# Adaptive-norm attention block with 16 heads on one core: q and k of a pair laid out through memory off chip in nine transfers, x kept on chip, scores 20 slots ahead

## The chip, the cores and the metric

One core of a Trainium2 chip. The metric is device time in microseconds (us): 351.57 us is the median of three runs of the kernel before (351.27 to 353.29). Engines: PE is TensorE, DVE is VectorE, ACT is ScalarE, POOL is GpSimd, SP is the queue that issues most DMAs. Each engine runs its own instructions in order; semaphores order the engines among each other.

## The reference

x is (16 batches, 256 tokens, 128), cut to what matters (f32 throughout):

```
mod = (silu(c) @ wmod)                 # per batch: sa, ca, ga, sb, cb, gb of 128 each; |ga|, |gb| >= 0.25
h   = layernorm(x) * (1 + ca) + sa
q, k, v = split(h @ W_qkv + b_qkv)     # 16 heads of 8
a   = softmax(q @ k^T over keys) / sqrt(128) @ v       # per batch and head, 256 x 256 scores
x   = x + ga * (a @ W_out + b_out)
h   = layernorm(x) * (1 + cb) + sb
x   = x + gb * (fp6(h) @ fp6(weight)^T + bias)         # fp6: blocks of 32 with a scale, rounded to e2m3
```

## The kernel before

Two batches make a **pair** (8 pairs). For a pair, `transpose_x`, `project_qk` and `save_qk` give q and k with the 128 channels on the partitions and 512 tokens in a row. The scores are products in float32r; to keep precision q and k are split into a high part (`save_qk` writes it) and a low part (`low_part`), and a head's product is taken over 96 rows: three heads, of each 8 channels in four combinations of high and low, with zeros in the rows of the other two. So q and k have to be **laid out**: `k_rep` holds groups of three (or two) heads in 96 rows, `q_pad` holds each head alone in its 32 rows of 96. SP does this with DMAs (`lay_out`): 6 of k and 16 of q for a pair, after two copies that double the parts. Rows 96 and 97 of `q_pad` take minus the row maximum of the scores (high and low part), which `place_max` brings by a DMA; the matching rows of `k_rep` are ones.

The work is a software pipeline in **steps**, one for each batch b, of 16 **slots** s. In slot s of step b PE does `scores1(b+1, s)` (scores of the next batch, whose maximum DVE takes in `maxima`), `scores2(b, s)` (the scores of this batch again, transposed and with the maximum subtracted, of which ACT takes the exponential), and, at some slots, `values` (probabilities times v), the projections of the batches b-1 and b-2, and the preparation of the pair two further on (odd steps: `transpose_x` at s=0, q at s=5, k at s=8). "Step 8" below is that of b = 8. POOL splits the maxima into high and low part (`split_max`), normalises x for a coming pair (`normalise1`, even steps; its inputs are the statistics that DVE takes in `stats1` at s=4 and `aggregate1` at s=5), modulates and quantises the second half of the block, and scales weights by the modulation of the batch (`attn_weights`, `ffn_weights`).

The way of a maximum of half a batch (8 heads): `maxima` (DVE), `split_max` (POOL), `transpose_max` (PE, into the one bank `ps_pre`), `save_maxT` (ACT), `place_max` (SP, DMA), then the first `scores2` of that half waits for it (`max_placed`). Half 0 of b+1 is transposed at s=11 of step b and needed at s=0 of step b+1; half 1 is transposed at s=2 of step b+1 and needed at s=8.

SP issues in a written order: in the step of an even b it starts with the layout of the next pair (22 DMAs), into which the two `place_max`, a store and a load of the modulation row (`load_modb`, two buffers) are put. x comes in twice for each pair (`x_early`, `x_late`). Four of the pair steps run in a loop of two rounds.

The lines: `lay_out` 313 to 326, `place_max` 398 to 402, SP's order 416 to 473, `split_max` 491, `normalise1` 499, POOL's order 539 to 574, `scores1` 865, `scores2` 878, `transpose_max` 933, PE's order 981 to 1043.

## Time and profile before

| | |
|---|---|
| median of three runs | 351.57 us |
| the profiled execution, first to last instruction | 349.2 us |
| PE busy | 304.0 us (87%) |
| DVE busy | 239.4 us (69%) |
| ACT busy | 218.5 us (63%) |
| POOL busy | 173.1 us (50%) |
| granted TensorE clock, mean | 0.908 |
| first exponential, last exponential ends | 45.4 us, 332.7 us |

The profiled execution is 2.4 us below the median. A matmul's end is modelled, so that busy PE means that matmuls are in flight, not that PE is at its peak. The granted clock is 1.00 at 2.4 GHz and 0.50 at 1.2 GHz. Windows below have the instructions of each engine in brackets behind its busy time.

### The profile page before, as it was taken

The page shows a single profiled execution, that of the slowest core. Times are in us where ns is not written, and L with a number is a line of the kernel's source. Part 1 is how long each engine was busy: PE and PEld are TensorE (multiplying, and loading weights), DVE is VectorE, ACT ScalarE, POOL GpSimd, SP SyncE. Part 2 cuts the span into 40 slices and gives each one's busy share as a digit, 9 for nine tenths or more (in the row PEclk, how much of TensorE's full clock was granted, in tenths as well). Part 3 has the DMA queues.
Part 4 walks back from the last instruction along what each step waited for, and adds up shares of the span by engine and source line. Part 5 has one row for each costly group of instructions (what it writes and reads, how often), then busy time and mean ns, then how long its engine had stood idle before and what let it go on. Part 6 is the DMA issues. An engine that isn't in the chain of part 4 may idle for free.

```text
span 349.2 us, 8125 instructions
## 1 busy us (share of the span) xinstructions
PE 304.0 (87%) x2506; PEld 216.6 (62%) x2506; DVE 239.4 (69%) x580; ACT 218.5 (63%) x404; POOL 173.1 (50%) x336
## 2 busy tenths in 40 slices
PE   3635698999899997999799997999899989999952
PEld 1204585767576765677576856677676758686521
DVE  4584587578856894779557992779677955886334
ACT  8683055876567765776477654776677645667720
POOL 4360133266736662566636672567556442546540
PEclk9955569999989998999899996999999987999995
DMA  4155365436552555345542555245544554001000
GB/s 132 32 110 115 112 178 111 113 110 174 107 132 93 159 107 122 104 154 101 112 100 94 168 116 120 90 151 103 113 126 139 107 109 126 32 19 34 18 17 15
DMA packets 23700, 36.46 MB, mean 104 GB/s; under 512 B 3422, under 2 KB 10734, under 8 KB 23670
## 3 DMA queue, kind: packets, MB, share of 16 engines
q1 hardware_dynamic: 23302, 35.43, 40.4%
q0 software_dynamic: 368, 0.66, 1.1%
q8 instruction: 16, 0.26, 0.3%
q14 instruction: 14, 0.11, 0.1%
HBM read 9.25 MB, written 2.13 MB: 33 GB/s over the span
## 4 chain that ended last, share of the span: by engine, by line
PE 40%; SPq 29%; DMA 16%; POOL 4%; issue 4%; DVE 3%; ACT 2%; DVEq 0%; ACTq 0%; POOLq 0%
SPq L326 24%; PE ps_o L903 10%; PE ps_p L888 9%; PE ps_p L874 8%; DMA qk_parts<-qk_parts 7%; DMA q_pad<-maxT 7%; PE ps_pre L930 3%; POOL qk_parts L371 2%; SPq L412 2%; PE ps_post L960 2%; SPq L401 2%; PE ps_o L946 1%; PE ps_post L974 1%; PE ps_post L968 1%; DMA q_pad<-qk_parts 1%
## 5 line engine op out<-in xcount | busy, mean ns | idle before, releaser
L762 DVE TENSOR_REDUCE neg_max<-ps_p 128x2 f32<-128x512 f32 x256 | 167.3, 685 | 72.7 <-PE ps_p L874 72.3
L629 ACT ACTIVATE probs<-ps_p 128x512 f32<-128x512 f32 x256 | 145.6, 595 | 82.1 <-PE ps_p L888 79.9
L874 PE MATMUL ps_p<-k_rep,q_pad 96*128 96x256 f32 x512 | 128.2, 338 | 12.1 <-DMA q_pad<-qk_parts 11.7
L888 PE MATMUL ps_p<-q_pad,k_rep 98*128 98x256 f32 x512 | 108.4, 296 | 12.5 <-DMA q_pad<-maxT 12.5
L874 PEld LDWEIGHTS ps_p<-k_rep,q_pad 96*128 96x128 f32 x512 | 84.6, 205 | 46.4 <-issue 35.0
L888 PEld LDWEIGHTS ps_p<-q_pad,k_rep 98*128 98x128 f32 x512 | 82.5, 198 | 16.8 <-issue 14.1
L903 PE MATMUL ps_o<-probs,v_aug 128*32 128x256 f32 x1024 | 82.3, 407 | 0.2 <-ACT probs L629 0.2
L903 PEld LDWEIGHTS ps_o<-probs,v_aug 128*32 128x32 f32 x1024 | 22.6, 112 | 20.2 <-issue 3.1
L530 POOL TENSOR_TENSOR wout_b<-wout_sc,modb 128x128 f32<-128x128 f32 x16 | 7.3, 459 | 49.7 <-DMA modb<-mod_rows_dram 49.6
L494 POOL CAST max_parts<-neg_max 128x16 fp32r<-128x16 f32 x32 | 6.3, 198 | 39.9 <-DVE neg_max L762 39.2
L356 POOL TENSOR_TENSOR hq<-h,rs 128x256 fp8e4<-128x256 f32 x15 | 9.3, 617 | 25.0 <-DVE rs L808 12.8
L371 POOL TENSOR_TENSOR qk_parts<-qk_full_sb,qk_parts 128x512 fp32r<-128x512 f32 x14 | 18.0, 1284 | 6.8 <-ACT qk_parts L610 6.8
L930 PE MATMUL ps_pre<-hT,wqkv_sb 128*128 128x512 f32 x28 | 16.0, 653 | 2.7 <-ACT hT L596 2.7
L621 ACT ACTIVATE maxT<-ps_pre 16x256 fp32r<-16x256 f32 x32 | 11.7, 365 | 10.6 <-PE ps_pre L937 10.6
L513 POOL TENSOR_TENSOR rstd<-ve,minus_half 128x2 f32<-128x2 f32 x16 | 11.3, 706 | 13.3 <-DVE ve L690 13.3
L503 POOL TENSOR_TENSOR rstd<-ve,minus_half 128x4 f32<-128x4 f32 x8 | 8.2, 1023 | 16.8 <-DVE ve L690 16.8
L633 ACT ACTIVATE oT<-ps_o 128x512 f32<-128x512 f32 x16 | 9.6, 598 | 9.4 <-PE ps_o L903 9.4
L506 POOL TENSOR_SCALAR xhat<-x_early,nm,rstd 128x128 f32<-128x128 f32 x32 | 14.1, 452 | 1.1 <-POOL rstd L503 0.7
L342 POOL TENSOR_SCALAR xh<-x,nm,rstd 128x128 f32<-128x128 f32 x30 | 13.2, 452 | 2.1 <-POOL rstd L513 1.4
L604 ACT ACTIVATE qk_full_sb<-ps_pre,bqkv_col 128x512 f32<-128x512 f32 x14 | 9.6, 688 | 7.1 <-PE ps_pre L930 7.1
L782 DVE TENSOR_TENSOR x<-ps_post,x_res 128x256 f32<-128x256 f32 x16 | 6.7, 421 | 10.6 <-PE ps_post L960 10.6
L968 PE MATMUL ps_post<-ident,hd 128*128 128x128 f32 x32 | 8.3, 347 | 6.1 <-DVE hd L359 6.1
(107 smaller groups left out, 356.1 us busy)
## 6 DMA issues: line engine op xcount, KB each, us to landing
q_pad<-qk_parts SPq DMA_DIRECT2D x123, 64.0 KB
qk_parts<-qk_parts SPq DMA_DIRECT2D x14, 512.0 KB, 3.5
k_rep<-qk_parts SPq DMA_DIRECT2D x31, 192.0 KB
modb<-mod_rows_dram SPq DMA_DIRECT2D x16, 256.0 KB, 3.7
x_early<-in_L_attn_x_dram SPq DMA_DIRECT2D x8, 256.0 KB, 3.4
x_late<-in_L_attn_x_dram SPq DMA_DIRECT2D x8, 256.0 KB, 3.4
out_dram<-out_sb SPq DMA_DIRECT2D x16, 128.0 KB, 1.9
k_rep<-qk_parts SPq DMA_DIRECT2D x15, 128.0 KB
```

Source lines behind the costliest of these rows:

```text
L326: eng.dma_start(dst.bitcast(F32), src).then_inc(landed[g], 16)
L342: ins = eng.tensor_scalar(xh2[:, n, :], x1[:, n, :], nm2[:, n:n + 1], rstd2[:, n:n + 1], ALU.add, ALU.mult)
L371: ins = eng.tensor_tensor(qk_parts[:, par, kind, 1 + kind, :], qk_full_sb[:, kind, :], qk_parts[:, par, kind, 0, :].bitcast(F32), ALU.subt ...
L506: ins = pool.tensor_scalar(xhat[:, n, :], x_early[:, n // 2, n % 2, :], nm1[:, n:n + 1], rstd1[:, n:n + 1], ALU.add, ALU.mult)
L621: act.activation(maxT[:, half, :], ps_pre[0:16, 0:T], ACT.Copy).then_inc(maxT_saved, 1)
L629: act.activation(probs[:, v % 2, u % 4, :], ps_p2[:, u % 2, :], ACT.Exp).then_inc(exp_done, 1)
L762: dve.tensor_reduce(neg_max[:, half, :, h % HALF], ps_p1[:, P1_BANK[h], :].rearrange("p (q k) -> p q k", q=QT), AX_X, ALU.max, negate=True ...
L874: ins = pe.matmul(ps_p1[:, P1_BANK[h], t * T:(t + 1) * T], q_pad[0:ROWS, par, h, e, t * P:(t + 1) * P], k_rep[0:ROWS, par, g, e, :], start ...
L888: ins = pe.matmul(ps_p2[:, u % 2, t * T:(t + 1) * T], k_rep[0:ROWS + 2, par, g, e, t * P:(t + 1) * P], q_pad[0:ROWS + 2, par, h, e, :], st ...
L903: ins = pe.matmul(ps_o[32 * j:32 * j + 32, half * T:(half + 1) * T], at[:, 2 * D * r:2 * D * r + 32], probs[:, v % 2, j, t * T:(t + 1) * T ...
L930: pe.matmul(bank[:, :], wqkv_sb[:, kind * E:(kind + 1) * E], hT[:, par, :], start=True, stop=True).then_inc(full, 1)
L968: ins = pe.transpose(ps_post[:, t * P:(t + 1) * P], hd[:, t, :], ident[:, :])
```

## The change

- `k_rep` and `q_pad` become `k_rows` and `q_rows`, a ring of two pairs as before, with 96 rows for a product and two more for the maximum. Head h now lies in band r = h mod 3 of 32 rows, and k's group is h // 3.
- The layout goes by way of memory off chip. `store_parts` writes q (one DMA of 1 MB) and k (two DMAs of 512 KB) with their doubled parts to `parts_dram`; `lay_out` reads them back, three DMAs for q and three for k, each into one band of 32 rows, with 320 or 384 KB. That is 9 DMAs for a pair where 24 were. The copies inside `qk_parts` are gone. The writes are issued in the odd step in which the pair is prepared, the reads at the beginning of the even step behind it.
- x is loaded once, in three DMAs at the start, and stays (`x_all`). The modulation rows have four buffers in place of two.
- `scores1` and `maxima` run 20 slots ahead of `scores2` in place of 16, in the order of heads that `scores2` has, over three banks in turn. In slot s of step b it is `scores1` of slot 16(b+1) + s + 4. A pair's first `scores1`, which waits for all six of its reads, so stands at s=12 of an even step.
- The maxima of half 0 and of half 1 of b+1 are transposed at s=8 and s=14 of step b (before: s=11, and s=2 of step b+1), and k is projected at s=10 (before: s=8).
- POOL's order: `normalise1` of an even step comes ahead of `attn_weights` and `split_max(b+1, 0)`; `split_max(b+1, 1)` follows `modulate2` of the same step (before: it began the next one).
- At the start ACT fills both rings of `q_rows` with zeros, the second between the preparation of pair 0 and that of pair 1; POOL fills `k_rows` with ones, the second between the norms of pair 0 and pair 1. The DMAs of POOL are gone. All loops are unrolled.

The core of the diff:

```diff
-ROWS = 96
-NREP = 11
...
+ROWS1 = 96
+ROWS2 = 98
+LEAD = 20
+RING = 2
+MODB_RING = 4
+P1_BANKS = 3
...
+    parts_dram = nc.dram_tensor("parts_dram", [NPAIR, 2, 3 * GROUPS * D, 4, TP], F32, kind="Internal").ap()
...
+            sp.dma_start(x_all[:, 4:NB, :, :], x_tok[:, 4:NB]).then_inc(x_in[2], 16)
...
+            def store_parts(p, kind):
+                wait(sp, (low_ready, 2 * p + 1 + kind))
+                if kind == 0:
+                    src = qk_parts[:, p % 2, 0, :, :].bitcast(F32).unsqueeze(1).to_broadcast([P, 2, 2, TP])
+                    sp.dma_start(parts_dram[p, 0, 0:P].rearrange("a (u v) t -> a u v t", v=2), src
+                                 ).then_inc(parts_stored[0], 16)
+                else:
+                    for part in range(2):
+                        src = qk_parts[:, p % 2, 1, part:part + 1, :].bitcast(F32).to_broadcast([P, 2, TP])
+                        sp.dma_start(parts_dram[p, 1, 0:P, 2 * part:2 * part + 2, :], src
+                                     ).then_inc(parts_stored[1], 16)
+            def lay_out(p, kind):
+                wait(sp, (parts_stored[kind], 16 * (1 + kind) * (p + 1)), (p2_full, 16 * 2 * (p - RING + 1)))
+                if p < RING:
+                    sp.wait_ge(rows_filled[p], 2)
+                by_row = parts_dram[p, kind].rearrange("(g r d) q t -> r (d q) g t", r=3, d=D)
+                for r in range(3):
+                    at = slice(32 * r, 32 * r + 32)
+                    dst = q_rows[at, p % RING, r::3, :, :] if kind == 0 else k_rows[at, p % RING, 0:HEADS_AT[r], :, :]
+                    sp.dma_start(dst.rearrange("a i e t -> a i (e t)").bitcast(F32), by_row[r][:, 0:HEADS_AT[r], :]
+                                 ).then_inc(laid_out[p % RING], 16)
...
-                if has_batch(b0):
-                    load_modb(b0, 0)
-                if has_pair(p + 1):
-                    wait(sp, (parts_copied, after(p + 1, 32, total=NPAIR - 1)), (p2_full, after(b0, 16)))
-                    if isinstance(p, int) and p == -1:
-                        sp.wait_ge(low_ready, 2)
-                        sp.wait_ge(pads_dve, 1)
-                    if isinstance(p, int) and p == 0:
-                        sp.wait_ge(pads_act, 2)
-                    lay_out(sp, 1 - par, 0, 0, 4)
-                if has_batch(b0):
-                    place_max(b0, par, 0, 1)
...
-                    lay_out(sp, 1 - par, 1, 0, 4 if first else 2)
-                if has_batch(b0 + 1):
-                    place_max(b0 + 1, par, 1, 0)
...
+                if late is not None:
+                    lay_out(late, 0)
+                    lay_out(late, 1)
+                if has(b + 1) and b >= 0:
+                    load_modb(b + 1)
+                if has(b - 2):
+                    store(b - 2)
+                if has(b + 1):
+                    place_max(b + 1, 0)
+                if early is not None:
+                    store_parts(early, 0)
+                    store_parts(early, 1)
+                if has(b + 1):
+                    place_max(b + 1, 1)
...
-            def pair_step(p, b0, par):
-                for e in range(2):
-                    b = b0 + e
-                    if isinstance(b, int) and b == 0:
-                        pool.wait_ge(const_ready, 1)
-                    if has_batch(b):
-                        split_max(b, 1)
-                    if has_batch(b - 2):
-                        residual2(b - 2)
-                    if has_batch(b):
-                        attn_weights(b, p, e)
-                    if has_batch(b - 1):
-                        ffn_weights(b - 1, 1 - e)
-                    if e == 0 and has_pair(p + 2):
-                        normalise1(p + 2, 0)
-                    if e == 1 and has_pair(p + 2) and not (isinstance(p, int) and p == -2):
-                        low_part(pool, p + 2, par, 0, q_saved)
-                    if has_batch(b + 1):
-                        split_max(b + 1, 0)
-                    if has_batch(b - 1):
-                        invert_deviation(b - 1)
-                        if not is_last(b - 1):
-                            modulate2(pool, b - 1, 1 - e)
-                    if e == 0 and has_pair(p + 2):
-                        normalise1(p + 2, 1)
-                    if e == 1 and has_pair(p + 2) and not (isinstance(p, int) and p == -2):
-                        low_part(pool, p + 2, par, 1, k_saved)
-                    if has_batch(b - 1) and not is_last(b - 1):
-                        quantise(pool, b - 1)
...
+                if has(b - 2):
+                    residual2(b - 2)
+                if norm_pair(b) is not None:
+                    normalise1(norm_pair(b), 0)
+                if has(b):
+                    attn_weights(b)
+                if has(b + 1):
+                    split_max(b + 1, 0)
+                if has(b - 1):
+                    ffn_weights(b - 1)
+                if low_pair(b) is not None:
+                    low_part(pool, low_pair(b), 0, q_saved)
+                if norm_pair(b) is not None:
+                    normalise1(norm_pair(b), 1)
+                if has(b - 1):
+                    invert_deviation(b - 1)
+                    if b != NB:
+                        modulate2(pool, b - 1)
+                if has(b + 1):
+                    split_max(b + 1, 1)
+                if low_pair(b) is not None:
+                    low_part(pool, low_pair(b), 1, k_saved)
+                if has(b - 1) and b != NB:
+                    quantise(pool, b - 1)
+                if b == -4:
+                    pool.memset(k_rows[:, 1, :, :, :].bitcast(F32), 1.0).then_inc(rows_filled[1], 1)
...
-                        if s == 2 and has_batch(b):
-                            transpose_max(b, 1, (hT_saved, after(p + 2 + e, 2, total=NPAIR)),
-                                          (maxT_saved, after(b, 2, 1)))
...
-                        if s == 11 and has_batch(b + 1):
-                            transpose_max(b + 1, 0, (k_saved, after(p + 2 + e, 2, total=NPAIR)),
-                                          (maxT_saved, after(b + 1, 2)), (v_saved, after(b + 2)))
...
+                    if s == 8 and has(b + 1):
+                        transpose_max(b + 1, 0, (q_saved, 2 * (pre + 1) if pre is not None else 0), (v_saved, b + 2))
+                    if s == 10 and pre is not None:
+                        if pre < 2:
+                            project_qk(pre, 1, k_full, ps_post, (modT_ready, 1), (k_saved, 2 * pre))
+                        else:
+                            project_qk(pre, 1, k_full, ps_pre, (maxT_saved, 2 * b + 3))
+                    if s in (9, 11) and has(b):
+                        values(b, 1, [(s - 9) // 2])
+                    if s == 14 and has(b + 1):
+                        transpose_max(b + 1, 1, (k_saved, 2 * (pre + 1) if pre is not None else 0),
+                                      (maxT_saved, 2 * b + 3))
```

Where instructions stand, first on PE in an even step, from s=7 on (`L874` and `L888` are `scores1` and `scores2`, `L903` is `values`, `L937` is `transpose_max`). Before:

```order
L903 MATMUL ps_o<-probs,v_aug 32x256 x4
L874 MATMUL ps_p<-k_rep,q_pad 128x256 x2
L888 MATMUL ps_p<-q_pad,k_rep 128x256 x2
L874 MATMUL ps_p<-k_rep,q_pad 128x256 x2
L888 MATMUL ps_p<-q_pad,k_rep 128x256 x2
L903 MATMUL ps_o<-probs,v_aug 32x256 x4
L874 MATMUL ps_p<-k_rep,q_pad 128x256 x2
L888 MATMUL ps_p<-q_pad,k_rep 128x256 x2
L874 MATMUL ps_p<-k_rep,q_pad 128x256 x2
L888 MATMUL ps_p<-q_pad,k_rep 128x256 x2
L903 MATMUL ps_o<-probs,v_aug 32x256 x4
L937 MATMUL ps_pre<-ident_r,max_parts 16x128 x2
```

After (`L792` and `L807` are the scores, `L822` is `values`, `L856` is `transpose_max`):

```order
L822 MATMUL ps_o<-probs,v_aug 32x256 x4
L792 MATMUL ps_p<-k_rows,q_rows 128x256 x2
L807 MATMUL ps_p<-q_rows,k_rows 128x256 x2
L856 MATMUL ps_pre<-ident_r,max_parts 16x128 x2
L792 MATMUL ps_p<-k_rows,q_rows 128x256 x2
L807 MATMUL ps_p<-q_rows,k_rows 128x256 x2
L822 MATMUL ps_o<-probs,v_aug 32x256 x4
L792 MATMUL ps_p<-k_rows,q_rows 128x256 x2
L807 MATMUL ps_p<-q_rows,k_rows 128x256 x2
```

The transposition of the maxima of half 0 has moved from behind the scores of s=11 to behind those of s=8. 

POOL in an even step (`rstd` of 128x4 and `xhat` are `normalise1`, `max_parts` is `split_max`, `rstd` of 128x2 begins the modulation of the second norm, `wout_b`, `bias_b`, `x_res` are `attn_weights`, `x1b` is `residual2`). Before, where `attn_weights` stands just ahead of these rows:

```order
L518 TENSOR_TENSOR wf_b<-wfT,modb 128x128 [waits x1b_ready,f_full]
L519 TENSOR_TENSOR bffn_b<-bffn_bc,modb 128x128
L503 TENSOR_TENSOR rstd<-ve,minus_half 128x4 [waits xT_full,stats1_ready]
L506 TENSOR_SCALAR xhat<-x_early,nm,rstd 128x128 [waits rstd1_ready]
L506 TENSOR_SCALAR xhat<-x_early,nm,rstd 128x128
L494 CAST max_parts<-neg_max 128x2x8 [waits maxT_full,max_done]
L496 TENSOR_TENSOR max_parts<-neg_max,max_parts 128x2x8 [waits max_high]
```

After:

```order
L461 TENSOR_TENSOR x1b<-x,bffn_b 128x256 [waits out_ready,bffn_b_ready]
L439 TENSOR_TENSOR rstd<-ve,minus_half 128x4 [waits xT_full,stats1_ready]
L442 TENSOR_SCALAR xhat<-x_all,nm,rstd 128x128 [waits rstd1_ready]
L442 TENSOR_SCALAR xhat<-x_all,nm,rstd 128x128
L467 TENSOR_TENSOR wout_b<-wout_sc,modb 128x128 [waits y_full,modb_in0]
L469 TENSOR_TENSOR bias_b<-attn_bias,modb 128x128
L472 TENSOR_TENSOR x_res<-x_all,bias_b 128x256 [waits x1_ready,x_rest_in,bias_b_ready]
L430 CAST max_parts<-neg_max 128x2x8 [waits maxT_full,max_done]
L432 TENSOR_TENSOR max_parts<-neg_max,max_parts 128x2x8 [waits max_high]
L454 TENSOR_TENSOR wf_b<-wfT,modb 128x128 [waits x1b_ready,f_full]
```

`attn_weights` has moved from ahead of `normalise1` to behind its first half, so that `normalise1` and `attn_weights` both lie ahead of `split_max`, and nothing but `residual2` lies ahead of `normalise1`.

SP from the beginning of an even step. Before:

```order
L326 DMA k_rep<-qk_parts 96x1x512 [waits p2_full,parts_copied]
L326 DMA q_pad<-qk_parts 32x1x512 x3
L401 DMA q_pad<-maxT 2x8x256 [waits maxT_saved]
L326 DMA k_rep<-qk_parts 96x1x512
L326 DMA q_pad<-qk_parts 32x1x512 x3
L326 DMA k_rep<-qk_parts 64x1x512
L326 DMA q_pad<-qk_parts 32x1x512 x2
L412 DMA out_dram<-out_sb 128x256 [waits out_ready]
L326 DMA k_rep<-qk_parts 96x1x512
L326 DMA q_pad<-qk_parts 32x1x512
L401 DMA q_pad<-maxT 2x8x256 [waits maxT_saved]
```

After:

```order
L367 DMA q_rows<-parts_dram 32x6x512 [waits p2_full,q_parts_stored]
L367 DMA q_rows<-parts_dram 32x5x512 x2
L367 DMA k_rows<-parts_dram 32x6x512 [waits p2_full,k_parts_stored]
L367 DMA k_rows<-parts_dram 32x5x512 x2
L380 DMA modb<-mod_rows_dram 128x512
L385 DMA out_dram<-out_sb 128x256 [waits out_ready]
L373 DMA q_rows<-maxT 2x8x256 [waits maxT_saved] x2
L380 DMA modb<-mod_rows_dram 128x512 [waits bffn_b_ready,wf_b_ready,h2_ready]
L385 DMA out_dram<-out_sb 128x256 [waits out_ready]
L373 DMA q_rows<-maxT 2x8x256 [waits maxT_saved]
L350 DMA parts_dram<-qk_parts 256x1x1024 [waits low_ready]
```

The `place_max` of half 0 of the next batch (before: the last row shown) had 13 layout DMAs ahead of it; now each `place_max` has the six reads of 32 rows ahead of it or the three writes behind it.

## Rows read from the trace of the kernel before

**Rows 1.** Page, part 1 and part 4: busy time with instructions; the chain by line.

```profile
PE 304.0 (87%) x2506; PEld 216.6 (62%) x2506; DVE 239.4 (69%) x580; ACT 218.5 (63%) x404; POOL 173.1 (50%) x336
...
SPq L326 24%; PE ps_o L903 10%; PE ps_p L888 9%; PE ps_p L874 8%; DMA qk_parts<-qk_parts 7%; DMA q_pad<-maxT 7%; PE ps_pre L930 3%; POOL qk_parts L371 2%; SPq L412 2%; PE ps_post L960 2%; SPq L401 2%; PE ps_o L946 1%; PE ps_post L974 1%; PE ps_post L968 1%; DMA q_pad<-qk_parts 1%
```

**Rows 2.** Waits: engine, line, what it waited for: us, times, longest.

```profile
PE ps_p L888 <- DMA q_pad<-maxT: 12.5, 7, 2.6
```

**Rows 3.** Chain that ended last, 230 to 250 us: start, us, what.

```profile
233.94 0.88 SPq L326
...
246.42 2.93 DMA q_pad<-maxT
```

**Rows 4.** Timeline, PE: start, us, engine, line, op, tiles [idle before].

```profile
211.30 0.76 PE L888 MATMUL ps_p<-q_pad,k_rep 98*128 98x256 f32 x2 [2.57 <-DMA q_pad<-maxT]
...
249.49 0.47 PE L888 MATMUL ps_p<-q_pad,k_rep 98*128 98x256 f32 x2 [1.21 <-DMA q_pad<-maxT]
```

**Rows 5.** Windows: length, busy PE, PEld, DVE, ACT, POOL, then PEclk, DMA share, GB/s.

```profile
61.00:300.00 239.00, 227.43 (x1974) 165.14 (x1974) 172.84 (x417) 158.69 (x315) 131.30 (x250) 0.95 0.48 119
211.30:216.90 5.60, 5.60 (x32) 4.05 (x33) 0.87 (x2) 3.08 (x6) 0.00 (x0) 0.50 0.63 149
```

**Rows 6.** Windows: steps 8, 11 and 14.

```profile
192.60:208.60 16.00, 16.00 (x154) 11.90 (x153) 14.36 (x40) 10.78 (x22) 11.02 (x22) 1.00 0.58 138
249.50:267.80 18.30, 18.30 (x160) 13.11 (x161) 12.19 (x28) 14.24 (x28) 9.53 (x18) 1.00 0.41 116
304.50:320.10 15.60, 15.60 (x153) 11.59 (x152) 12.89 (x29) 10.74 (x22) 8.20 (x17) 1.00 0.08 27
```

**Rows 7.** Timeline, step 8, of POOL, DVE and PE.

```profile
196.53 0.46 POOL L530 TENSOR_TENSOR wout_b<-wout_sc,modb 128x128 f32<-128x128 f32 x1 [1.19 <-DMA modb<-mod_rows_dram]
197.49 0.73 POOL L536 TENSOR_TENSOR x_res<-x_late,bias_b 128x256 f32<-128x256 f32 x1
200.02 0.16 DVE L690 TENSOR_SCALAR ve<-mv 128x4 f32<-128x4 f32 x1
200.26 1.02 POOL L503 TENSOR_TENSOR rstd<-ve,minus_half 128x4 f32<-128x4 f32 x1 [1.21 <-DVE ve L690]
201.54 0.47 PE L888 MATMUL ps_p<-q_pad,k_rep 98*128 98x256 f32 x2
202.62 0.23 POOL L496 TENSOR_TENSOR max_parts<-neg_max,max_parts 128x16 fp32r<-128x16 f32 x1
203.32 0.70 POOL L513 TENSOR_TENSOR rstd<-ve,minus_half 128x2 f32<-128x2 f32 x1 [0.47 <-DVE ve L690]
204.70 0.29 PE L937 MATMUL ps_pre<-ident_r,max_parts 128*16 128x128 f32 x2
205.97 0.73 POOL L349 TENSOR_TENSOR h<-xm,modb 128x256 f32<-128x256 f32 x1
```

**Rows 8.** Windows: DMA while a 128-row copy runs, and while the layout runs.

```profile
231.40:233.90 2.50, 2.50 (x33) 1.56 (x32) 2.43 (x7) 1.77 (x4) 1.38 (x3) 1.00 0.86 278
233.90:255.90 22.00, 20.79 (x199) 16.27 (x192) 17.69 (x47) 14.83 (x32) 11.89 (x24) 1.00 0.57 126
```

**Rows 9.** Page, part 6: a load from memory off chip, issue to landing.

```profile
modb<-mod_rows_dram SPq DMA_DIRECT2D x16, 256.0 KB, 3.7
```

**Rows 10.** Timeline of the start: ACT, DVE, PE; first exponentials of steps 0 and 2.

```profile
2.54 7.01 ACT L585 ACTIVATE q_pad<-ident 128x8192 fp32r<-128x8192 f32 x1
17.19 1.23 DVE L367 TENSOR_TENSOR qk_parts<-qk_full_sb,qk_parts 128x1024 fp32r<-128x1024 f32 x1 [0.26 <-ACT qk_parts L606]
29.13 1.62 PE L874 MATMUL ps_p<-k_rep,q_pad 96*128 96x256 f32 x6 [8.12 <-DMA q_pad<-qk_parts]
45.39 0.60 ACT L629 ACTIVATE probs<-ps_p 128x512 f32<-128x512 f32 x1 [3.39 <-PE ps_p L888]
...
79.24 1.08 ACT L629 ACTIVATE probs<-ps_p 128x512 f32<-128x512 f32 x2 [0.62 <-PE ps_p L888]
```

**Rows 11.** Windows: the start, 30 to 49.8 us.

```profile
30.00:49.80 19.80, 15.84 (x66) 13.85 (x66) 14.13 (x26) 4.00 (x8) 3.66 (x8) 0.50 0.54 141
```

More of the change, by code:

```diff
@@ L375, in adaln_block, with low_part @@
+        def low_part(eng, p, kind, saved):
+            wait(eng, (saved, 2 * p + 2))
+            eng.tensor_tensor(qk_parts[:, p % 2, kind, 1, :], qk_full_sb[:, kind, :],
+                              qk_parts[:, p % 2, kind, 0, :].bitcast(F32), ALU.subtract).then_inc(low_ready, 1)
         block = ctx.enter_context(nc.Block())
@@ new lines, in place_max, with load_modb @@
+            def place_max(b, half):
+                wait(sp, (maxT_saved, 2 * b + half + 1))
+                sp.dma_start(q_rows[ROWS1:ROWS2, b // 2 % RING, 8 * half:8 * half + 8, b % 2, :].bitcast(F32),
+                             maxT[:, half, :].bitcast(F32)).then_inc(max_placed[half], 16)
+            def load_modb(b):
+                was = b - MODB_RING + 1
+                wait(sp, (h2_ready, was), (wf_b_ready, was), (bffn_b_ready, was))
+                sp.dma_start(modb[:, b % MODB_RING, :, :].rearrange("p a n -> p (a n)"),
+                             mod_rows_dram[b:b + 1, :].to_broadcast([P, 4 * E])).then_inc(modb_in[b % MODB_RING], 16)
@@ L597, in save_hT, with save_qk @@
                                    scale=scaleT[:, col], bias=shiftT[:, col]).then_inc(hT_saved, 1)
-            def save_qk(p, par, kind, full, saved, bank=ps_pre):
-                wait(act, (full, after(p + 1, total=NPAIR)), (low_ready, after(p, 2, total=NPAIR)),
-                     *[landed(g, p - 1) for g in range(len(GROUPS))])
+            def save_qk(p, kind, full, saved, bank=ps_pre):
+                wait(act, (full, p + 1), (low_ready, 2 * p), (parts_stored[kind], 16 * (1 + kind) * (p - 1)))
@@ L789, in stats2 @@
             def stats2(b):
-                wait_apart(dve, (st2_done, after(b + 1)))
+                wait(dve, (st2_done, b + 1))
                 for n in range(QT):
@@ L893, in values, with before_scores1, scores1 @@
-            def values(b, e, v, tiles=range(QT)):
+            pe.wait_ge(wqkv_loaded, 16 * 4)
+            def before_scores1(b, s):
+                wait(pe, (max_done, 16 * b + s + 1 - P1_BANKS))
+                if s == 0 and b % 2 == 0:
+                    wait(pe, (laid_out[b // 2 % RING], 96 * (b // 2 // RING + 1)))
+            def scores1(b, s, t):
+                h = HEAD[s]
+                slot, e = b // 2 % RING, b % 2
+                ins = pe.matmul(ps_p1[:, (16 * b + s) % P1_BANKS, t * T:(t + 1) * T],
+                                q_rows[0:ROWS1, slot, h, e, t * P:(t + 1) * P],
+                                k_rows[0:ROWS1, slot, h // 3, e, :], start=True, stop=True)
+                if t == QT - 1:
+                    ins.then_inc(p1_full, 1)
@@ new lines, in before_scores2, with scores2 @@
+            def before_scores2(b, u):
+                wait(pe, (exp_done, 16 * b + u - 1))
+                if u % HALF == 0:
+                    wait(pe, (max_placed[u // HALF], 16 * (b + 1)))
+            def scores2(b, u, t):
+                h = HEAD[u]
+                slot, e = b // 2 % RING, b % 2
+                ins = pe.matmul(ps_p2[:, u % 2, t * T:(t + 1) * T],
+                                k_rows[0:ROWS2, slot, h // 3, e, t * P:(t + 1) * P],
+                                q_rows[0:ROWS2, slot, h, e, :], start=True, stop=True)
+                if t == QT - 1:
+                    ins.then_inc(p2_full, 1)
```

669 lines of the change are left out of this document (274 added, 395 removed).

## Prediction

> **What bounds the kernel now.** The page comes first: PE is busy 87% of the span, but 24% of the chain that ended last is SP issuing the layout [rows 1]. So I looked in the waits for the place where the two meet. PE waits 12.5 us in all, seven times, for the DMA that places the maxima, at the first `scores2` of an odd step [rows 2]. The chain shows why: from 233.94 on SP issues 13 layout DMAs at 0.7 to 1.1 us each, and only at 246.42 the `place_max` on which PE waits; it lands 2.93 us later [rows 3]. Two of these waits in the timeline are 2.57 and 1.21 us long, and they are 38.2 us apart, one pair [rows 4].
>
> The waits cost more than their length. Behind the one of 2.57 us the granted clock is 0.50 (1.2 GHz) for 5.6 us, with 32 matmuls where step 8 has 154 in 16.0 us, so 54 in 5.6 us: some 2.3 us are lost, 0.41 of the time at that clock [rows 5, 6]. From 61 to 300 us the mean clock is 0.95, so 24 us at 1.2 GHz, of which 0.41 is 9.8 us [rows 5]. That is 1.4 us for each wait. Waits and slow clock together are 22 us.
>
> Without them PE is continuously busy: an even step takes 16.0 us (step 8), an odd one with the preparation of a pair 18.3 us (step 11), step 14, with nothing to prepare, 15.6 us [rows 6]. DVE and ACT have idle time in each of these. So PE sets the pace, and a stall in its own order is not made up.
>
> **The change, part by part.**
>
> *SP's queue and the maxima.* 9 layout DMAs for 24, and half 0 is transposed at s=8, eight slots ahead of its use, not five. A `place_max` takes 2.9 us [rows 3]; eight slots are about half of a 16.0 us step, so that even with 2 us behind other DMAs it is there. The seven waits go: -12.5 us and about -9.8 us of slow clock.
>
> *POOL's order against the earlier transposition.* This is the new wait that I expect. PE reaches `transpose_max(b+1, 0)` directly after the scores of s=8. In step 8 these end at 202.0 [rows 7]. `split_max` must have been done by then. In POOL's new order `normalise1`, `attn_weights` and then `split_max` follow each other, and `normalise1` cannot start before DVE's `aggregate1` of s=5, whose last instruction ends at 200.2 [rows 7]; nothing in the change makes that earlier. From the start of `rstd` at 200.26 to the end of `split_max` at 202.85 are 2.59 us, and `attn_weights`, which was done ahead of it (196.53 to 198.22, 1.69 us), is now in between [rows 7]: the split ends at 204.54. PE waits 2.5 us. Before, the transposition came at 204.70 [rows 7], 1.8 us after the split, and this chain was hidden. Behind the waiting matmul stand all of PE's scores, and ACT and DVE behind them. It happens in each even step with a `normalise1`: steps 0, 2, 4, 6, 8, 10, six times. Odd steps have no `normalise1`, and POOL is in time.
>
> A wait of this length is like that of rows 4; I take 1.7 us for the clock behind it, between the mean of 1.4 and the 2.3 of the nearest row; the ends are 0 and 2.3. An even step so becomes 16.0 + 2.5 + 1.7 = 20.2 us.
>
> The second split of an even step, `split_max(b+1, 1)`, has `ffn_weights`, half of `xhat` and the modulation ahead of it. The modulation takes from 203.32 to 206.70 [rows 7], the other two about 1.8 us by the same sizes (four instructions of 0.45 us, as `wout_b`): about 5.7 us after 204.5 with the split itself, 210.2. PE reaches s=14 some 5.3 us of work and 1.7 us of slow clock behind 204.5. It is just hidden. If the clock doesn't fall, up to 0.4 us of this come back as a wait.
>
> *Layout through memory.* For a pair 2.1 MB are written and 2.1 MB read, where 1 MB was copied and 2.1 MB laid out. No row shows 1 MB going to memory off chip; the nearest rates are 278 GB/s (copies over 128 rows) and 126 GB/s (the old layout, with SP issuing) [rows 8]. A load of 256 KB takes 3.7 us [rows 9], of which 0.9 at 278 GB/s, so some 2.8 us are fixed, issue included. The reads start with the even step, after the last `scores2` that uses the buffer. At 278 GB/s they are done 2.8 + 7.6 = 10.4 us into the step, at 126 GB/s 19.5 us. They are needed at s=12: that slot follows the transposition at 204.70, so 12.4 us into the step, and 4.2 us later, at 16.6 us, with the new wait. I take the fast end, since the sources are no longer the few rows of 8 channels that the old DMAs read: no cost. The writes end before: q's is issued after s=8 of the odd step, k's by the end of `low_part`, about 1.5 us before the step ends, and they land some 3 us into the next, while q's reads run.
>
> The Trainium skill ("SBUF — State Buffer", Door 1: The DMA port swizzle) says that partitions 0 to 31, and also 0 to 63, reach only 8 of the 16 ports, and gives 189 GB/s measured for a transfer of 1 MiB into 32 rows. By it the reads would take 11 us (an estimate from that page) and be in time with the new wait, a little late without it. No row shows a read of this kind.
>
> *Start.* The first `scores1` came at 29.1, after low parts that were ready at 18.4 [rows 10]. The doubled rows of `qk_parts` are not written any more (two instructions of 1024 elements each become 512 on ACT and on DVE), which gives about 1.5 us. But the round trip is in the path: q out by 21, k out by 23 to 25, both back by about 32 (7.6 us at 278 GB/s for the reads from 21.5 on, and 2.8 us). ACT's second fill of 7.0 us [rows 10] now lies ahead of pair 1; PE projects k of pair 1 by about 28, so it stays behind the 32. Then 20 slots, not 16, before step 0. The start before took 16.3 us from 29.1 to the first exponential at 45.4 [rows 10], at 1.2 GHz with waits in between [rows 11]; without these four more slots find room. I take 46.0, with 42 and 50 as ends.
>
> *Steps 0 and 1* took 33.8 us (45.4 to 79.2) [rows 10]. The slow clock up to 49.8 goes (4.4 us, 0.41 of it: -1.8) [rows 11], so does one average wait (-1.8), and the new wait with its clock comes (+4.2): 34.4.
>
> *The end.* Four slots less of `scores1` in step 14: 0.2 us of PE each, -0.8. The rest as before: from 320.5 to 349.2, 28.7.
>
> *At nothing:* x loaded once and four modulation buffers (POOL's wait for `modb` was idle time of an engine with more), unrolling (steps in the loop and outside it are alike in length).
>
> **The sum**, against the profiled 349.2: 46.0 + 34.4 + 5 x 20.2 (steps 2 to 10) + 5 x 18.3 (3 to 11) + 2 x 16.0 (12, 13) + 14.8 + 28.7 = 348.4. The median of the runs is 2.4 above the profiled time, so 350.8. In short, seven waits at the pair's boundary are exchanged for six inside the even steps.
>
> **Rivals.**
> - *The clock doesn't fall behind the new wait.* The rows show it falling behind 2.57 us but not in step 11, whose wait was 1.21. Then 6 x 1.7 less: 340.6. Chance 16%.
> - *The new wait does not reach PE,* because the statistics come earlier in a pipeline that no longer stalls. Against it: DVE takes them behind PE's `transpose_o` and `linear` of s=3, a fixed place of the step. Then 6 x 4.2 less: 325.6, if the reads land within 12.4 us. Chance 10%.
> - *Slower: the reads are late.* At the 126 GB/s of rows 8 they land at 19.5, 2.9 us after they are needed, six times, each with 1.7 of clock: +27, 378. It decides below 2.1 MB in the 13.8 us that are left (16.6 less 2.8), 152 GB/s. Chance 10%.
> - *Slower: a late start* (first exponential at 50, the end above), with pair 1's layout late in step 0 since it is written behind the maxima of batch 0: +4 and +4, 359. Chance 12%.
>
> **How the numbers follow.** The forecast has 52%; within it 38% lie within 1% (348 to 355, what a measurement of this kernel can tell from no change), 7% on either side. Faster: 7 + 16 + 10 = 33%. Slower: 7 + 10 + 12 = 29%. The range leaves out 325.6 and 378 and takes in the others: 339 to 362.
>
> **What would show it.** PE idle 2.5 us before `transpose_max` in steps 0 to 10, even ones only, with `max_parts` of POOL as releaser; a clock of 0.50 behind it; even steps near 20, odd ones near 18.3, steps 12 and 13 near 16; no wait for `q_rows<-maxT`; all reads of a pair landed before s=12. A wait of PE for `q_rows<-parts_dram` or `k_rows<-parts_dram` beyond the first would make the prediction wrong upward, even steps of 16 us downward.

## The result, and the profile of the changed kernel

The changed kernel takes 388.23 us (median of 4 runs, 386.72 to 391.51), the kernel before 351.42 us in the same comparison: a ratio of 1.107, 95% interval 1.0998 to 1.1142. I had forecast 350.8 us with a range of 339 to 362. It is slower by 37 us, and above the range.

The profiled execution took 389.6 us. The page, parts 1 and 2 (busy time; 40 slices of the span with the granted clock in tenths):

```profile
PE 336.4 (86%) x2506; PEld 237.2 (61%) x2506; DVE 237.6 (61%) x579; ACT 219.3 (56%) x404; POOL 172.1 (44%) x330
...
PEclk9955676699759995799659985999669995999995
```

PE has as many instructions as before [rows 1] and 32 us more of busy time. The clock falls once in every even step up to step 12. The waits of PE (engine, line, tile, what it waited for: us, times, longest):

```profile
PE ps_pre L856 <- POOL max_parts L432: 14.6, 7, 2.5
...
PE ps_p L792 <- DMA k_rows<-parts_dram: 9.1, 3, 5.5
```

The waits for `q_pad<-maxT` [rows 2] have no successor: those are gone. In their place stands the wait for POOL's split. Timeline of step 6 (start, us, engine, line, op, tiles, idle before):

```profile
183.56 0.16 DVE L609 TENSOR_SCALAR ve<-mv 128x4 f32<-128x4 f32 x1
183.80 1.02 POOL L439 TENSOR_TENSOR rstd<-ve,minus_half 128x4 f32<-128x4 f32 x1 [5.63 <-DVE ve L609]
...
186.70 0.72 POOL L472 TENSOR_TENSOR x_res<-x_all,bias_b 128x256 f32<-128x256 f32 x1
...
187.65 0.22 POOL L432 TENSOR_TENSOR max_parts<-neg_max,max_parts 128x16 fp32r<-128x16 f32 x1
...
187.92 0.40 PE L856 MATMUL ps_pre<-ident_r,max_parts 128*16 128x128 f32 x2 [2.48 <-POOL max_parts L432]
```

POOL has been idle for 5.63 us when the statistics come, and then has `normalise1`, `attn_weights` and the split in a row while PE waits: the chain of the prediction, and its 2.5 us. What I had not foreseen stands in the windows of steps 8 and 9 (length, busy PE, PEld, DVE, ACT, POOL, then clock, DMA share, GB/s), and of the stretch at half clock (1.2 GHz) in step 6:

```profile
221.00:245.00 24.00, 21.52 (x153) 15.30 (x152) 14.63 (x40) 11.18 (x22) 12.27 (x25) 0.72 0.56 134
245.00:263.70 18.70, 18.70 (x163) 13.49 (x162) 13.04 (x30) 14.26 (x28) 9.13 (x17) 0.99 0.27 100
187.40:204.50 17.10, 16.58 (x93) 10.88 (x94) 6.80 (x12) 6.94 (x14) 8.92 (x20) 0.50 0.18 47
```

Step 9 is near the forecast (18.7 us for 18.3). The even step takes 24.0, not 20.2. Behind a wait of the kernel before the clock was at 0.50 for 5.6 us of the row shown [rows 5], and for 6.8 us in all, since the fall came within the wait; here it is for 17.1 us in step 6 and for 13.7 us in each of steps 0, 2, 4, 8 and 10. In steps 4, 6 and 10 the stretch reaches 3 to 4 us into the odd step behind, which then takes 19.8 to 20.1 us.

### The profile page after: what moved, and what is told of

Its sections match the earlier page's. It is cut to its first block, busy times and chain, and to the rows that moved or that the text cites. A ratio compares the mean times of both kernels' runs of the same rounds, so it can differ in the third digit from the quotient of the medians.

```text
span 389.6 us, 7131 instructions
## 1 busy us (share of the span) xinstructions
PE 336.4 (86%) x2506; PEld 237.2 (61%) x2506; DVE 237.6 (61%) x579; ACT 219.3 (56%) x404; POOL 172.1 (44%) x330
## 4 chain that ended last, share of the span: by engine, by line
PE 60%; DVE 8%; POOL 7%; DMA 7%; issue 3%; SPq 1%; ACT 1%; POOLq 0%; DVEq 0%
PE ps_o L822 17%; PE ps_p L792 17%; PE ps_p L807 14%; DMA k_rows<-parts_dram 5%; DVE neg_max L682 4%; PE ps_pre L849 3%; DMA parts_dram<-qk_parts 2%; PE ps_post L880 1%; PE ps_post L888 1%; POOL rstd L439 1%; PE ps_pre L833 1%; PE ps_pre L856 1%; PE ps_post L894 1%; PE ps_o L866 1%; DVE st L614 1%
## 5 line engine op out<-in xcount | busy, mean ns | idle before, releaser
L553 ACT ACTIVATE probs<-ps_p 128x512 f32<-128x512 f32 x256 | 148.7, 595 | 103.7 <-PE ps_p L807 102.4
L792 PE MATMUL ps_p<-k_rows,q_rows 96*128 96x256 f32 x512 | 141.9, 368 | 9.8 <-DMA k_rows<-parts_dram 9.1
L792 PEld LDWEIGHTS ps_p<-k_rows,q_rows 96*128 96x128 f32 x512 | 94.4, 229 | 58.9 <-DVE neg_max L682 29.6
L807 PE MATMUL ps_p<-q_rows,k_rows 98*128 98x256 f32 x512 | 117.4, 317 | 0.0
L807 PEld LDWEIGHTS ps_p<-q_rows,k_rows 98*128 98x128 f32 x512 | 92.9, 223 | 3.8 <-ACT probs L553 2.1
L822 PE MATMUL ps_o<-probs,v_aug 128*32 128x256 f32 x1024 | 92.5, 451 | 0.2 <-ACT probs L553 0.2
L822 PEld LDWEIGHTS ps_o<-probs,v_aug 128*32 128x32 f32 x1024 | 23.7, 118 | 22.2 <-issue 5.4
L321 POOL TENSOR_TENSOR qk_parts<-qk_full_sb,qk_parts 128x512 fp32r<-128x512 f32 x14 | 17.8, 1274 | 16.9 <-ACT qk_parts L534 16.9
L849 PE MATMUL ps_pre<-hT,wqkv_sb 128*128 128x512 f32 x28 | 16.9, 686 | 9.8 <-ACT hT L526 9.8
L856 PE MATMUL ps_pre<-ident_r,max_parts 128*16 128x128 f32 x64 | 10.5, 251 | 14.7 <-POOL max_parts L432 14.6
L545 ACT ACTIVATE maxT<-ps_pre 16x256 fp32r<-16x256 f32 x32 | 11.5, 360 | 18.3 <-PE ps_pre L856 18.3
L856 PEld LDWEIGHTS ps_pre<-ident_r,max_parts 128*16 128x16 f32 x64 | 6.3, 108 | 17.2 <-POOL max_parts L432 16.3
L442 POOL TENSOR_SCALAR xhat<-x_all,nm,rstd 128x128 f32<-128x128 f32 x32 | 14.0, 446 | 0.8
L511 ACT ACTIVATE q_rows<-ident 128x8192 fp32r<-128x8192 f32 x2 | 14.0, 7020 | 0.0
```

The lines of the kernel that those rows point to most:

```text
L321: eng.tensor_tensor(qk_parts[:, p % 2, kind, 1, :], qk_full_sb[:, kind, :], qk_parts[:, p % 2, kind, 0, :].bitcast(F32), ALU.subtract).the ...
L442: ins = pool.tensor_scalar(xhat[:, n, :], x_all[:, 2 * p + n // 2, n % 2, :], nm1[:, n:n + 1], rstd1[:, n:n + 1], ALU.add, ALU.mult)
L511: act.activation(q_rows[:, slot, :, :, :], ident[:, 0:1].to_broadcast([P, H * TP]).rearrange("p (i e t) -> p i e t", i=H, e=2), ACT.Copy, ...
L553: act.activation(probs[:, v % 2, u % 4, :], ps_p2[:, u % 2, :], ACT.Exp).then_inc(exp_done, 1)
L792: ins = pe.matmul(ps_p1[:, (16 * b + s) % P1_BANKS, t * T:(t + 1) * T], q_rows[0:ROWS1, slot, h, e, t * P:(t + 1) * P], k_rows[0:ROWS1, sl ...
L807: ins = pe.matmul(ps_p2[:, u % 2, t * T:(t + 1) * T], k_rows[0:ROWS2, slot, h // 3, e, t * P:(t + 1) * P], q_rows[0:ROWS2, slot, h, e, :], ...
```

## Experiments

Each ratio is to the kernel before, measured in the same comparison. The theories A, B, C, D, L and P are defined in the expectations, which were written before each run.

**POOL's order alone.** `attn_weights` and the split go ahead of `normalise1` again:

```diff
-                if norm_pair(b) is not None:
-                    normalise1(norm_pair(b), 0)
                 if has(b):
                     attn_weights(b)
                 if has(b + 1):
                     split_max(b + 1, 0)
+                if norm_pair(b) is not None:
+                    normalise1(norm_pair(b), 0)
```

> The changed kernel with one thing undone: on POOL, attn_weights and split_max of half 0 stand ahead of the first half of normalise1 again. Theory A (the wait for the split at s=8 starts the slow clock, and a second wait lies hidden behind it): the 2.5 us in even steps go, but the six reads of a pair land 13 to 14 us after the step begins (in step 6 at 190.0 after a beginning at 176.8) and are needed at about 12.4, so PE waits 1 to 3 us for k_rows<-parts_dram at s=12 in each of steps 0 to 12, and the clock falls behind that: 375 to 388 us. Rival B (the split's wait is all there is): six times 2.5 us of wait and 13.6 us at half clock, of which 0.43 is lost, come back: 338 us. Rival C (the clock is low for another reason than the wait, such as the four reads and writes running beside): the wait goes and the low stretches stay where they are: 373 us, with a low clock starting near s=8 or before.

Measured: 369.9 us, ratio 1.056 (1.0478 to 1.0644). 18 us come back, where the split's wait alone would have given 50. The wait for the split is gone, and behind it stands another (waits of PE):

```profile
PE ps_p L792 <- DMA k_rows<-parts_dram: 23.3, 8, 5.6
```

It is 2.3 to 2.6 us long at s=12 of steps 2, 4, 6 and 12, with 10.2 us of half clock behind each, but 1.04 and 1.34 us in steps 8 and 10, with none. The time lies 5 us below the range of theory A (375 to 388), which had the clock fall in all seven even steps, where it falls in five. C's 373 us is nearer, but C falls by the place: each stretch begins within a wait at s=12, not near s=8, and steps 8 and 10, with the same reads, have none. B falls.

**The reads by batch.** Each read is cut into the even and the odd batch of the pair, all of the even batch's six first, with a semaphore for each batch; the first `scores1` of a pair waits for half of the bytes:

```diff
-            def lay_out(p, kind):
+            def lay_out(p, kind, e):
...
-                    sp.dma_start(dst.rearrange("a i e t -> a i (e t)").bitcast(F32), by_row[r][:, 0:HEADS_AT[r], :]
-                                 ).then_inc(laid_out[p % RING], 16)
+                    sp.dma_start(dst.bitcast(F32), by_row[r][:, 0:HEADS_AT[r], e * T:(e + 1) * T]
+                                 ).then_inc(laid_out[p % RING][e], 16)
...
-                if s == 0 and b % 2 == 0:
-                    wait(pe, (laid_out[b // 2 % RING], 96 * (b // 2 // RING + 1)))
+                if s == 0:
+                    wait(pe, (laid_out[b // 2 % RING][b % 2], 96 * (b // 2 // RING + 1)))
```

> The changed kernel with each of the six reads of a pair cut into the two batches of the pair (12 reads, those of the even batch first, each batch with a semaphore of its own), POOL's order as changed. Theory A: only the wait for the reads in step 12 (2.8 us and 10.3 us at half clock) and that of step 0 go, the 2.5 us at s=8 stay in steps 0 to 10: 378 to 384 us. Rival C (the reads beside the matmuls cause the long low clock): over 10 us more than that come back, or low stretches move with the reads.

Measured: 373.5 us, ratio 1.070 (1.0623 to 1.0767), 4 us better than expected; the start gains most of that (first exponential at 44.2 us, not 49.0). The split's wait stays:

```profile
PE ps_pre L858 <- POOL max_parts L434: 15.0, 7, 2.5
```

The stretch at half clock behind it isn't always the same length: 3.4 us in step 0, then 6.8, 10.2, 13.7, 17.1 and 13.7 us in steps 2 to 10. Yet PE waits 2.35 us in step 0 and 2.49 us in all the others, and issues the same instructions behind. In step 2 the clock comes back with nothing but scores and `values` on PE (windows before and behind the rise):

```profile
93.10:99.80 6.70, 6.70 (x40) 4.05 (x40) 3.22 (x5) 2.97 (x5) 4.16 (x9) 0.50 0.13 38
99.90:102.10 2.20, 2.20 (x24) 1.58 (x21) 1.53 (x5) 1.33 (x3) 0.06 (x1) 1.00 0.00 0
```

**Both.**

> Both edits together: POOL's split ahead of normalise1, and the reads by batch. Theory A: no wait of over 1 us is left in steps 0 to 14, even steps of about 16.2 us, odd ones of 18.5, clock 1.00 in both: 49 + 15 x 17.1 + 12 + 17 = 330 to 340 us, under the kernel before. Rival C: 360 us or more, since the low clock stays without a wait. Against theory B, it has to be clearly faster than the kernel with POOL's order alone; by B the two are equal.

Measured: 330.8 us, ratio 0.9435 (0.9389 to 0.948). The two edits give 18 and 15 us apart and 57 together: either wait alone is enough to lose the clock for most of what is left of an even step, in most of these steps. In the steps one wait of over 1 us is left, 1.5 us for `q_rows<-maxT` in step 1, with 3.4 us at half clock. Steps 8 and 9, and all from 64 to 300 us:

```profile
184.40:201.10 16.70, 16.17 (x156) 11.96 (x155) 14.22 (x40) 10.91 (x23) 11.60 (x25) 1.00 0.77 187
201.10:219.50 18.40, 18.40 (x162) 13.19 (x161) 13.22 (x30) 14.11 (x29) 10.07 (x18) 1.00 0.29 109
64.10:300.00 235.90, 233.01 (x2121) 169.68 (x2119) 184.49 (x448) 167.21 (x336) 139.72 (x269) 1.00 0.48 132
```

**The waits of the kernel before.** To size the first term of the sum, the kernel before with one `place_max` ahead of two layout DMAs:

```diff
+                if has_batch(b0 + 1):
+                    place_max(b0 + 1, par, 1, 0)
                 if has_pair(p + 1):
                     lay_out(sp, 1 - par, 1, 0, 4 if first else 2)
-                if has_batch(b0 + 1):
-                    place_max(b0 + 1, par, 1, 0)
```

> The kernel before with one edit: in SP's order the place_max of half 0 of the odd batch comes ahead of the two layout DMAs that stood in front of it. It tests the first term of my sum, 12.5 us of waits and 9.8 us of slow clock behind them. If maxT is saved at 205.3 and the DMA takes 2.9 us it is in place at 208.2, before PE asks at 208.7. By my sum 351.4 - 22 = 329 to 333 us. Rival: the wait goes, but the layout DMAs behind it come late for the first scores of the next pair, and the time stays within 1% of 351.

Measured: 333.6 us, ratio 0.9514 (0.9463 to 0.9565): 17 us, not 22. The clock is 1.00 from 49.6 us to the last exponentials, and the wait is nearly gone:

```profile
PE ps_p L888 <- DMA q_pad<-maxT: 3.8, 8, 1.5
```

So of 12.5 us of waits and 9.8 of slow clock 8.7 and 9.8 were given back, less 1.6 us that I can't place; the other 3.8 us of waits are still in this kernel. The mechanism was right, and the size nearly.

**How long the clock stays low, and why.** Four kernels measure it by itself. Into the kernel with both edits a wait is put on purpose, the same in all but its place:

```diff
+            def probe(b):
+                wait(sp, (p2_full, 16 * b + 9))
+                sp.dma_start(probe_dram[b].rearrange("p (a n) -> p a n", a=4),
+                             ident[:, :].unsqueeze(1).to_broadcast([P, 4, P])).then_inc(probed, 16)
...
+                    if s == 8 and b in PROBED:
+                        pe.wait_ge(probed, 16 * (PROBED.index(b) + 1))
```

At s=8 of even steps (as shown):

> The version without waits (both edits, 330.8 us) with a wait put in on purpose: in steps 2, 4, 6, 8, 10 and 12, when scores2 of s=8 is done, SP stores 256 KB of ident to memory off chip (read by nobody), and PE waits for that store before it goes on; some 2.5 us each. Theory P (how long the half clock lasts hangs on where in the step it falls, since it rises only with the matmuls of 128 columns and more that begin the next step): about 13 us at half clock each, as behind the split's wait, so 330.8 + 6 x (2.5 + 0.43 x 11) = 375 us. Rival L (it hangs on the length of the wait or on chance, with 3.4 and 6.8 us as in the kernel before): 330.8 + 6 x (2.5 + 1.7) = 356 us.

The two runs took 398.8 and 407.1 us, too far apart for a ratio. The store landed 6.1 us after its issue (2.6 us in the run at s=8 of odd steps), with the reads issued just ahead of it, so that the wait was 5.5 to 6.7 us, not 2.5: it is no clean comparison of place. The half clock lasts 17.1 us once and 20.5 us five times, like this:

```profile
231.50:251.80 20.30, 16.27 (x92) 10.71 (x92) 6.80 (x12) 6.91 (x13) 7.04 (x14) 0.50 0.20 52
```

Behind the scores of s=0 of odd steps (`p2_full` 16b + 1):

> The same wait, of the same length, put behind the scores of s=0 in steps 3, 5, 7, 9, 11 and 13, where the kernel before had its waits. Theory P: 3.4 or 6.8 us at half clock behind each, as in the kernel before: 330.8 + 6 x (2.5 + 0.43 x 4) = 356 us. Rival L: the same time as with the wait at s=8. A third (the long low stretches of the changed kernel come from its reads and writes beside the matmuls): 10 us and more here too, 370 us.

362.3 us, ratio 1.031 (1.0187 to 1.0437); waits of 2.7 to 3.0 us, half clock for 6.8 us four times and 3.4 twice. That is P's mechanism, 6 us over its 356: the waits sum to 16.9 us, and 0.43 of 34.1 us at half clock is 14.7, so 362.4 from 330.8. At s=8 of odd steps:

> The same wait at s=8 of steps 3, 5, 7, 9, 11 and 13. By theory P it lasts until the next even step has begun, but k's projection at s=10 of steps 3 to 11 (512 columns) may bring the clock back earlier: between 5 and 13 us each, 356 to 375 us; where it lies tells whether one long matmul is enough. By L 356.

366.3 us, ratio 1.043 (1.0299 to 1.0553). This one tells most, since the six waits are equal, 2.70 to 2.74 us. In steps 3 to 11 the clock is back after 3.4 or 6.8 us; in step 13, the only one that has no k to project at s=10, after 17.1. Timeline of PE in step 11 and windows (just behind in step 11, then after it; step 13):

```profile
269.31 0.29 PE L870 MATMUL ps_pre<-ident_r,max_parts 128*16 128x128 f32 x2 [2.72 <-DMA probe_dram<-ident]
...
271.25 1.91 PE L863 MATMUL ps_pre<-hT,wqkv_sb 128*128 128x512 f32 x2
```

```profile
271.10:274.50 3.40, 3.40 (x17) 1.79 (x15) 1.39 (x2) 1.90 (x4) 0.12 (x1) 0.51 0.78 308
274.60:279.20 4.60, 4.60 (x45) 3.30 (x41) 3.38 (x8) 2.79 (x7) 2.09 (x3) 1.00 0.47 179
305.30:322.30 17.00, 15.79 (x89) 10.09 (x90) 6.80 (x12) 6.11 (x12) 6.44 (x13) 0.50 0.09 30
```

In step 13 PE is busy without a gap, once the wait is over, with scores, `values` and the transposition of maxima, and stays at 1.2 GHz; in step 11 one projection of 128x512 is among them, and the clock is back 3.4 us after it fell. Step 13 also has next to no transfers beside (DMA share 0.09 for 0.78), so the last word is with the run "One matmul more". Behind the scores of s=0 of even steps:

> The same wait behind the scores of s=0 in steps 2, 4, 6, 8, 10 and 12, where no pair is prepared. By theory P the dense work at s=1 to s=6 (values, transposition of o, v's projection, the linear layer) brings the clock back as in an odd step: 3.4 to 6.8 us each, 352 to 358 us. If only the preparation of a pair in odd steps brings it back, the low stretch goes on through the whole even step: 15 us each and 375 us or more.

366.4 us, ratio 1.043 (1.0303 to 1.0555). Waits of 3.3 to 3.6 us, 6.8 us of half clock in each: a step without the preparation of a pair brings the clock back too, if the wait comes ahead of its `values` and transpositions. The time is 8 us over the expectation; waits that are 0.8 us longer make 5 of it, and six stretches of 6.8 us, where those 358 us stand for 4.7 each, cover the rest.

**One matmul more.** The changed kernel, nothing undone, with a product that nobody reads:

```diff
+                    if s == 10 and b % 2 == 0 and 0 <= b <= 10:
+                        wait(pe, (maxT_saved, 2 * b + 3))
+                        pe.matmul(ps_pre[:, :], wqkv_sb[:, 0:E], hT[:, (b // 2 + 1) % 2, :], start=True, stop=True)
```

> The changed kernel (388.2 us) with nothing undone and one matmul more in each of steps 0, 2, 4, 6, 8 and 10: at s=10 a product of 128x512 float32 into the bank ps_pre that nobody reads (0.69 us at full clock, 1.3 at half). Theory P (the clock stays low behind the split's wait because scores and values alone don't bring it back, and one long matmul does, as k's projection did in steps 3 to 11 of the run with the wait at s=8 of odd steps): the low stretches in even steps shrink from 13.6 to 17 us down to 3.4 to 6.8, and the time falls by 6 x (0.43 x 8 - 1) = 15 us, to 372 or so, although PE has more to do and waits as long. Rival: the stretch is as long as before, and the matmuls cost 6 x 1.2 us: 395 us.

Measured: 375.1 us, ratio 1.063 (1.052 to 1.0741), 13 us faster than the changed kernel, with more work. PE in step 6, then the windows before and behind the rise:

```profile
179.30 0.40 PE L856 MATMUL ps_pre<-ident_r,max_parts 128*16 128x128 f32 x2 [2.48 <-POOL max_parts L432]
...
182.62 1.91 PE L952 MATMUL ps_pre<-hT,wqkv_sb 128*128 128x512 f32 x2
...
186.25 0.51 PE L792 MATMUL ps_p<-k_rows,q_rows 96*128 96x256 f32 x2
```

```profile
179.30:186.10 6.80, 6.80 (x32) 3.92 (x32) 2.08 (x3) 2.16 (x4) 4.89 (x11) 0.50 0.29 69
186.20:190.70 4.50, 4.50 (x45) 3.33 (x42) 3.40 (x8) 2.46 (x6) 0.67 (x2) 1.00 0.00 0
```

The wait is as long as before (2.48 us), the half clock lasts 6.8 us in steps 2 to 10 where it was 13.7 or 17.1. All four runs (371.0 to 377.6 us) lie below the fastest of the changed kernel (386.7). So a 128x512 product behind the wait shortens the stretch. That nothing else does isn't shown: the reads by batch had short ones without it.

**The rate of the reads.** POOL's order undone, and k read in 96 rows for five of its six groups, in 32 for the last:

```diff
+                if kind == 1:
+                    by_row = parts_dram[p, kind].rearrange("(g r d) q t -> (r d q) g t", r=3, d=D)
+                    for rows, first, last in ((96, 0, 5), (32, 5, 6)):
...
```

> The kernel with POOL's order undone (369.9 us, which waits 1.0 to 2.6 us for k_rows at s=12 in steps 2 to 12, four times with the clock behind), and k read in one DMA of 96 rows by 5 groups and one of 32 rows in place of three of 32 rows; the bytes are the same. My sum took the reads at 278 GB/s, the rate of copies over 128 rows; the six reads ran at 209 to 219. Theory D (the number of rows of a DMA sets its rate): k's reads are done 1 to 1.5 us earlier, PE waits about 1 us or less, the clock doesn't fall behind it: 342 to 350 us. Rival (the rate is that of the sum of all packets, whatever the rows): as late as before, 368 to 372 us.

Measured: 358.9 us, ratio 1.024 (1.0115 to 1.0359), 11 us faster than with three bands of 32 rows, though above the 342 to 350 expected; its slowest run (364.5 us) lies below the fastest of the other kernel (368.2). While the reads run, in step 6 of the kernel with POOL's order alone, and of this one:

```profile
178.00:185.00 7.00, 5.40 (x54) 3.64 (x50) 5.47 (x20) 3.24 (x7) 5.89 (x11) 1.00 1.06 215
```

```profile
171.00:177.00 6.00, 4.98 (x49) 3.25 (x48) 5.07 (x16) 3.01 (x6) 5.30 (x11) 1.00 1.04 242
```

The waits are 0.9 to 1.8 us in steps 2 to 12. The clock fell behind 1.78 and 1.58, not behind 1.59 (step 12) and shorter ones. The runs scatter (353.0 to 364.5 us); the traced one is the fastest, and why the others are slower isn't shown. In the kernel of "POOL's order alone" with scores 19 slots ahead (`LEAD = 19`) it scatters too:

> The kernel with POOL's order undone and scores1 19 slots ahead in place of 20, so that the six reads are needed at s=13, one slot or some 1.1 us later, with half a slot's row less of work ahead. Theory A: the waits for k_rows, 2.3 to 2.6 us where the clock fell and 1.0 to 1.3 where it didn't, become 1.2 to 1.5 and below 0.3; the clock falls in one or two steps at most: 340 to 350 us. Rival (the time is set by when the reads land and the slot doesn't matter): 366 to 370.

366.3 us (359.8 to 371.0), which can't be told from the kernel with 20 slots (368.2 to 377.1). A miss: the waits were 1.1 to 1.7 us in steps 2 to 10, but the clock fell behind three of these (1.71, 1.74 and 1.21) and not behind 1.68 and 1.10.

**Both edits and k in 96 rows.**

> The version without waits (POOL's order undone, reads by batch of the pair, 330.8 us), with k read in 96 rows as well (10 reads for a pair in place of 12). By the run with 96 rows the reads of the even batch land about 0.6 us earlier, but nothing waits for them in steps 2 to 12; only the first scores can gain. 329 to 331 us, a ratio of about 0.94 to the kernel before. Against it: if the rate of the reads also slows PE's or the maxima's DMAs beside them, the gain is larger, 326 us; if the DMAs of 96 rows by 1 KB pieces are worse, 333.

331.95 us, ratio 0.9427 (0.9378 to 0.9475): the same as with both edits. Where nothing waits for the reads, their rate is worth nothing.

## Why the prediction was wrong

Against the sum of 348.4, for the profiled 389.6:

| term | forecast | measured | difference |
|---|---|---|---|
| first exponential | 46.0 | 49.0 | +3.0 |
| steps 0, 1 | 34.4 | 41.8 | +7.4 |
| steps 2, 4, 6, 8, 10 | 101.0 | 118.3 | +17.3 |
| steps 3, 5, 7, 9, 11 | 91.5 | 97.5 | +6.0 |
| steps 12, 13 | 32.0 | 39.0 | +7.0 |
| step 14 and the end | 43.5 | 44.0 | +0.5 |

A step counts from its first exponential to that of the next.

- **The waits at the pair's boundary go: right.** No wait for `q_rows<-maxT` is left in the changed kernel. In the kernel before, one DMA moved gave 17 us of the 22, with 3.8 us of the waits still there.
- **The new wait at the transposition of s=8: right**, in its place (steps 0 to 10, even ones), its releaser and its length: 2.48 to 2.49 us in steps 2 to 10 against 2.5 (2.0 in step 0).
- **"I take 1.7 us for the clock behind it": wrong, and this decides.** I had priced the clock by the length of the wait, from rows at the beginning of odd steps. The same wait costs more or less by what PE issues behind it, and not by that alone. In steps 2 to 10 of the changed kernel 60.5 us lie at half clock, and 11.2 in steps 3 to 11. The loss is 0.43 of them: two slots take 3.02 us at half clock and 1.72 at full (the `scores1` at 190.22 and 193.24 of the changed kernel, at 186.25 and 187.97 of the one with the matmul more). That is 26 us and 4.8, against the 8.5 of the sum. Each wait cost 6.2 us of slow clock in place of 1.7. The difference, 17.5 and 4.8, is the third and most of the fourth row of the table. A warning stood in the trace. Behind the wait of 2.57 us in [rows 4] PE transposes x at once, while in the order given for the change only scores and `values` stand behind the transposition at s=8. The row behind that wait, in the kernel before:

```profile
211.86 1.05 PE L915 MATMUL ps_pre<-ident,xhat 128*128 128x128 f32 x4
```

It would have told that the two places differ, but not the length: in the reads by batch the same order left 3.4 to 17.1 us. Why they differ is open.
- **"I take the fast end" for the reads: wrong.** They ran at 215 to 229 GB/s (below for the changed kernel), not 278, and landed 13 to 14 us into the step. The 16.6 us that the new wait gave them hid that in steps 2 to 10. It shows in step 12, which has no such wait (2.83 us for `k_rows`, 10.2 us of half clock), in step 0 (0.7 us), and at the start, where the reads landed at 35.0, not 32. With k read over 96 rows they went at 242 GB/s. The Trainium skill ("SBUF — State Buffer", Door 1: The DMA port swizzle) gives 189 GB/s for a transfer of 1 MiB into 32 rows, from which the prediction had an estimate of 11 us. The trace is nearer to that than to my 278.

```profile
178.00:189.00 11.00, 8.52 (x74) 7.07 (x70) 7.91 (x28) 5.70 (x12) 5.10 (x12) 0.93 1.02 229
```

- **Steps 0 and 1.** I had the slow clock of the start end before them. It went on from 49.0 to 54.3 us, and with the 13.7 us behind the wait that makes 18.9 us at half clock, 8 us lost.
- **The rivals.** "The clock doesn't fall" and "the new wait does not reach PE" are refuted. "The reads are late" had the right second wait, hidden by the first. Of "a late start" the first part came true (49.0 us, where its end is 50). None had a longer stretch at half clock, and the bound "0 and 2.3" for it was taken from one row: the range was too narrow above for that reason.

## What to carry to other kernels

Price a wait of TensorE by its place too, not by its length alone. Ahead of scores and `values` only, 2.5 us cost some 8 us in most steps (2.5 and 0.43 of 13.7). Where a 128x512 product came soon after, they cost 4 to 5.4 us (2.5 and 0.43 of 3.4 or 6.8). When one wait has been found, look for the next need behind it, with the time the first one lends taken away: here two waits in one step each kept the loss alive, and only undoing both gave 57 us. A transfer that is cut so that its first user waits for its own half only takes the rate off the path, for six more issues a pair.
